# The low parts of the turned tiles: made by GpSimd from a raw copy in SBUF, where VectorE made them from PSUM

## The reference

```python
x = x + tanh(g_xattn[0]) * L0_xattn(ctx, layernorm(x), ...)   # 32 half-heads of 8, att0 - lam * att1
x = x + tanh(g_ffn[0])   * L0_ffn(layernorm(x), ...)          # top 3 of 8 zones, gelu(x @ Wa[e]) @ Wb[e]
x = x + tanh(g_xattn[1]) * L1_xattn(layernorm(x), ctx, ...)   # 16 heads of 16, then @ Wo + bo
x = x + tanh(g_ffn[1])   * L1_ffn(layernorm(x), ...)          # silu(x @ wg.T) * (x @ wu.T) @ wd.T

def layernorm(x):  return (x - mean(x)) / sqrt(var(x) + 1e-5)
```

## Time and profile before

| | |
|---|---|
| median of three runs | 722.27 us |
| profiled execution | 724.65 us |
| its span, first to last instruction | 722.8 us |
| PE busy | 641.1 us (89%) |
| DVE busy | 368.1 us (51%), 814 instructions |
| ACT busy | 370.6 us (51%), 627 instructions |
| POOL busy | 114.3 us (16%), 158 instructions |
| mean granted clock of PE | 0.92 of full |

### The profile page before, as it was taken

How to read it: one execution, slowest core, us unless ns; L and a number is a source line. 1 busy time by engine, 2 the same in 40 slices (tenths; PEclk the granted TensorE clock), 3 DMA queues, 4 the chain that set the end, 5 groups by cost and what they waited for, 6 DMA issues and landing times.

```text
span 722.8 us, 10171 instructions
## 1 busy us (share of the span) xinstructions
PE 641.1 (89%) x3676; PEld 487.8 (67%) x3676; DVE 368.1 (51%) x814; ACT 370.6 (51%) x627; POOL 114.3 (16%) x158
## 2 busy tenths in 40 slices
PE   2377798888889999999999999999888879999996
PEld 2354455545448788888888777787566657888885
DVE  6447566586575352534536535434446655443332
ACT  4124465655666574646657535545753655333332
POOL 8000434334462000000000000000021313000000
PEclk9757899998779999999999999999888878999999
DMA  7301111023003021030203240000161100000000
GB/s 221 87 3 44 46 47 47 18 65 100 3 29 117 2 79 38 0 117 1 89 29 89 64 141 2 1 1 2 26 197 42 47 2 2 0 30 1 29 30 29
DMA packets 22737, 34.66 MB, mean 48 GB/s; under 512 B 4640, under 2 KB 13216, under 8 KB 22688
## 3 DMA queue, kind: packets, MB, share of 16 engines
q1 hardware_dynamic: 21376, 32.87, 15.1%
q10 hardware_dynamic: 864, 0.86, 0.5%
q0 software_dynamic: 448, 0.29, 0.4%
HBM read 18.93 MB, written 2.10 MB: 29 GB/s over the span
## 4 chain that ended last, share of the span: by engine, by line
PE 74%; DVE 8%; ACT 5%; SPq 4%; issue 3%; DMA 3%; POOL 2%; ACTq 1%; DVEq 0%; POOLq 0%
PE SC L1127 27%; PE PV L1127 25%; PE PV L1145 5%; PE SC L1258 4%; PE AUX L1127 4%; PE AUX L1230 3%; DVE NM L1011 3%; SPq L521 2%; SPq L532 2%; DMA QG<-NMT 2%; PE AUX L1186 2%; ACT XN L729 1%; DVE O L1019 1%; ACTq L712 1%; ACT NMT L770 1%
## 5 line engine op out<-in xcount | busy, mean ns | idle before, releaser
L871 DVE TENSOR_TENSOR HL<-HF,HH 128x512 fp32r<-128x512 f32 x120 | 83.3, 695 | 156.2 <-ACT HH L823 156.0
L781 ACT ACTIVATE PB<-SC 77x1024 f32<-77x1024 f32 x96 | 95.1, 1014 | 63.7 <-PE SC L1258 63.3
L823 ACT ACTIVATE HH<-PV 128x512 fp32r<-128x512 f32 x96 | 57.3, 597 | 66.7 <-PE SC L1127 66.7
L1258 PE MATMUL SC<-QG,KA 128*128 128x512 f32 x192 | 75.2, 487 | 16.0 <-DMA QG<-NMT 14.0
L818 ACT ACTIVATE HF<-PV 128x512 f32<-128x512 f32 x96 | 57.5, 599 | 58.4 <-PE PV L1127 56.3
L1127 PE MATMUL PV<-XH,WAH 128*128 128x512 f32 x192 | 78.2, 407 | 1.0 <-DVE O L1019 1.0
L1127 PE MATMUL PV<-XL,WAH 128*128 128x512 f32 x192 | 76.4, 398 | 0.0
L1127 PE MATMUL PV<-XH,WAL 128*128 128x512 f32 x192 | 76.2, 397 | 0.0
L1127 PE MATMUL SC<-HL,WBH 128*128 128x512 f32 x192 | 75.6, 394 | 0.0
L1127 PE MATMUL SC<-HH,WBH 128*128 128x512 f32 x192 | 75.3, 392 | 0.0
L1127 PE MATMUL SC<-HH,WBL 128*128 128x512 f32 x192 | 75.0, 390 | 0.0
(11 more groups left out here) (236 smaller groups left out, 1190.8 us busy)
## 6 DMA issues: line engine op xcount, KB each, us to landing
QG<-QH SPq DMA_DIRECT2D x120, 64.0 KB, 2.0
WSA<-in_wa SPq DMA_DIRECT2D x6, 1024.0 KB, 4.9
WSB<-in_wb SPq DMA_DIRECT2D x12, 512.0 KB, 6.8
QG<-QL SPq DMA_DIRECT2D x60, 64.0 KB, 2.0
X<-in_x SPq DMA_DIRECT2D x4, 512.0 KB, 6.0
out_x<-X SPq DMA_DIRECT2D x4, 512.0 KB, 2.6
WI<-in_wg SPq DMA_DIRECT2D x1, 768.0 KB, 4.4
WI<-in_wu SPq DMA_DIRECT2D x1, 768.0 KB, 6.8
```

Of the source, the lines that this page charges most:

```text
L781: act.activation(probs(n)[0:S, :, :], SC[0:S, n % 2, :, :], ACT.Exp, scale=SCALE[a]).then_inc(exp_done, 1)
L823: act.activation(HH[s % 2][:, :], PV[:, s % 2, :], ACT.Gelu_apprx_tanh).then_inc(act_done, 1)
L871: return dve.tensor_tensor(dst, raw, hi.bitcast(F32), ALU.subtract)
L1258: ins = pe.matmul(SC[:, n % 2, i, :], KALL[a][:, at_h:at_h + P], QG[m % 2][:, h // NS[a], :], start=True, stop=True)
```

## The change

ACT, which copied each half once, now copies it twice: first raw into `XN` (the buffer that the transposes have just read), then rounded into `XH`. The rounded copy frees the bank. Since the raw copies overwrite `XN`, ACT waits until both halves are transposed before it starts. POOL then subtracts, `XL = XN - XH`, from SBUF, and counts a new semaphore `lo_ready`. The users of a turned tile on PE wait for `lo_ready` (`turned`), and so does the next `scale`, which writes `XN` again. DVE has no part in `turn` any more; `turn_mix` keeps its old form.

```diff
+        def turned(eng, stage, j):
+            eng.wait_ge(lo_ready, KC * (order["turn", stage, j] + 1))
 # gpsimd
+                elif kind == "turn":
+                    _, stage, j = step
+                    for c in range(KC):
+                        pool.wait_ge(hi_ready, KC * order[step] + c + 1)
+                        used(pool, step + (c,))
+                        raw = XN[:, KC * c:KC * (c + 1), :].rearrange("p t n -> p (t n)")
+                        lo_part(XL[:, j, c, :], raw, XH[:, j, c, :]).then_inc(lo_ready, 1)
 # scalar
                     for c in range(KC):
                         filled(act, step + (c,))
+                    for c in range(KC):
                         pooled = {"accum_out": POOLED[:, c, j:j + 1]} if stage == FFN0 else {}
-                        act.activation(XH[:, j, c, :], bank(step + (c,)), copy, **pooled).then_inc(hi_ready, 1)
+                        raw = XN[:, KC * c:KC * (c + 1), :].rearrange("p t n -> p (t n)")
+                        act.activation(raw, bank(step + (c,)), copy).then_inc(hi_ready, 1)
+                        act.activation(XH[:, j, c, :], bank(step + (c,)), copy, **pooled).then_inc(frees(step + (c,)), 1)
                 elif kind == "scale":
...
                     if n:
-                        filled(act, ("turn",) + NORMS[n - 1][1:] + (KC - 1,))
+                        act.wait_ge(lo_ready, KC * n)
 # vector
-                elif kind == "turn":
-                    _, stage, j = step
-                    for c in range(KC):
-                        key = step + (c,)
-                        dve.wait_ge(hi_ready, KC * order[step] + c + 1)
-                        lo_part(XL[:, j, c, :], bank(key), XH[:, j, c, :]).then_inc(frees(key), 1)
 # tensor: query, and in the same way route 0, zone and gated
-                    for c in range(KC):
-                        used(pe, ("turn", ATT1 if a else ATT0, j, c))
+                    turned(pe, ATT1 if a else ATT0, j)
```

More of the change, by code:

```diff
@@ L436, in flamingo @@
         var_ready, rstd_ready, xn_ready = sem("var_ready"), sem("rstd_ready"), sem("xn_ready")
-        hi_ready, qh_ready = sem("hi_ready"), sem("qh_ready")
+        hi_ready, qh_ready, lo_ready = sem("hi_ready"), sem("qh_ready"), sem("lo_ready")
         gates_done, lam_sum, lam_exp, coef_done = (sem(n) for n in ("gates_done", "lam_sum", "lam_exp", "coef_done"))
@@ L1268, in _ @@
                     cols = [(c, 2 * b + i) for c in range(KC) for i in range(2)]
-                    for c in range(KC):
-                        used(pe, ("turn", FFN0, 2 * b + 1, c))
+                    turned(pe, FFN0, 2 * b + 1)
                     for i, (c, j) in enumerate(cols):
@@ L1283, in _ @@
                     if z % TOPK == 0 and f == 0:
-                        for c in range(KC):
-                            used(pe, ("turn", FFN0, j, c))
+                        turned(pe, FFN0, j)
                     if nt == 0:
@@ L1334, in _ @@
                         pe.wait_ge(fsplit_done, 2)
-                        for c in range(KC):
-                            used(pe, ("turn", FFN1, j, c))
+                        turned(pe, FFN1, j)
                     if s >= 2:
```

## The result

The four runs of the changed kernel took 740.48, 741.01, 743.48 and 830.90 us, median 742.25, against 722.83 us (median of four) for the kernel before. The ratio is 1.0255, 95% interval 1.0212 to 1.0298: 18.4 us slower (15.3 to 21.5). Ratios leave out executions more than 1.5% above the fastest of their kernel, here the one of 830.90 us at a granted clock of 0.72 (the other three have a median of 741.01) and further on one each in runs 5 and 6 (there the profiled one) and two in run 7, while the medians count them. The forecast was 740.0 in a range of 729 to 747.

What follows compares the result with a forecast made beforehand. PE was taken as nearly full in the zones, with room in ATT0's attention, where low parts' latency counts. Terms sum to 17.75 us, taking the profiled 724.65 to 742.4; against the 722.27 median, 740.0; range 729 to 747.

Steps and rivals of the forecast that it cites:

- First query: ATT0 tile 0: POOL's subtractions stand behind its small DMAs; 2.9 us stall plus 2.4 of slow query, 5.3.
- Tile 1: ATT0 tile 1: four copies free the second bank later for the maxima; 0.5 us, bounds -1.0 to 1.0.
- Tile 2: ATT0 tile 2: query waits 1.7 us for low parts, then runs at the low clock, 2.4 more; 4.1.
- Tile 3: ATT0 tile 3: norm's power late behind POOL's subtractions 1.1, query's wait 1.7, low clock 2.4; 5.2 us.
- Route: FFN0 tile 1: PE's first route waits for `lo_ready`; 1.45 us, bounds 0 and 3.5.
- End of ATT0: FFN0 tile 2's turn: two raw copies on ACT, which is on the chain there; 1.1 us, bounds 0 and 2.
- ATT1's tile 2: ATT1's tile 2 query: low parts come later, clock left out; 1.1 us, bounds 0.8 and 3.5.
- Nine other turns, and HL: Remaining turns: copies in ACT's waits, subtractions covered by PE's products; 0 in sum, bounds -2 and 3; HL delay a rival.
- The third rival: POOL's subtractions hold up DVE's HL in six turns of zones and gated part: 7.7 us more, 747.7; chance 0.07.
- DVE's relief: Subtractions taken off DVE shorten PE's waits for maxima in attention; -1.0 us, bounds 0 and -8.4.
- The rival in which it decides: Start and attention: DVE's saved 13.7 us all shorten the chain, the clock stays up; 720.1 us, chance 0.09.
- a clock that stays up: ATT0's three stalled queries: no low clock follows, so 3 x 2.4 = 7.2 us go; 732.8, chance 0.20.

Runs made afterwards that it cites:

- run 5: Changed kernel, but DVE instead of POOL subtracts the high part from the raw copy in SBUF: 736.5 us, ratio 1.0198.
- run 6: Changed kernel without the raw copies, POOL subtracting from the untransposed tile, so XL holds wrong numbers: 736.2 us, ratio 1.0162.
- run 7: Kernel before plus ACT's raw copies, which nobody reads; DVE still subtracts from PSUM: 733.9 us, ratio 1.0132.
- run 4: Changed kernel, but POOL issues its 13 small DMAs behind the first tile's two subtractions: 741.8 us, ratio 1.0233.
- run 1: Late turns alone: kernel before with only the eight turns of ATT1 and FFN1 changed: 724.4 us, ratio 1.0007.
- run 3: The hybrid: kernel before with only the eight turns that have no user close behind changed: 721.6 us, ratio 0.9978.
- run 10: Kernel before with filling matmuls on PE ahead of waits for moved maxima, three stalls actually filled: 720.6 us, ratio 0.9951.
- run 11: Kernel before with the eight turns that have time changed, plus filling matmuls ahead of waits for moved maxima: 720.0 us, ratio 0.9968.
- run 9: Changed kernel; routes wait for high parts alone, and FFN0 tile 0's update of X stands behind tile 3's power: 735.5 us, ratio 1.0163.
- run 12: Changed kernel, all turns on POOL, with every remedy: subtractions before DMAs, two waits off, stalls filled: 728.1 us, ratio 1.0077.
- run 8: Changed kernel with PE filling matmuls ahead of the queries of ATT0's tiles 0, 2 and 3: 735.4 us, ratio 1.0179.

## Why the prediction was right, and where not

The time came out 1 to 2 us above the forecast and the likeliest case, stalls with a slow PE behind them, is the one that came. Of its terms some were right and some met their size by luck. Measured against the trace of before, cut at the same instructions:

*First query.* Predicted 5.3, as 2.9 of stall and 2.4 of slow matmuls. Measured 5.35: 2.8 more idle, 2.6 more busy. Right in both parts; that most of the stall is owed to POOL's DMAs is shown by run 4.

*Tile 1.* Predicted 0.5; to the second query's QH the lag grew by 0.03, with 0.7 more idle and 0.6 less busy. Right in idle time.

*Tile 2.* Predicted 1.7 + 2.4 = 4.1. Measured 2.8: 1.5 idle, 1.3 busy. The query began fast and was slow only from its third matmul to its tenth, so the clock's price was too high here. The stall looks right, but in part by luck: the old code waits 0.09 us at this query in the trace of before and 1.50 in its other four (runs 1, 3, 10, 11), and it needs 41.2 us for this stretch in the first and 41.6, 43.8 and 41.7 in runs 1, 3 and 10.

*Tile 3.* Predicted 1.1 + 1.7 + 2.4 = 5.2. Measured 6.3: 2.6 idle, 3.7 busy. The sum is near, the step is another: not the query's wait (1.18, not 1.7) put PE to the slow level, but the wait for XN that the late power brought (2.88), one query earlier. Run 9 takes that wait away, and half of the 6.3 goes. The old code alone, in runs 1, 3 and 10, needed 47.5 us for this stretch where the trace of before has 44.78: a slow spell early in it lasts 14 us there and 4 in before. The changed kernel's trace has the short spell too, and run 4's, with the long one, needs 54.16. Like against like the stretch grows by 6.3 and by 6.6 us.

*Route.* Predicted 1.45 of waiting. The step fails as put: PE waited 0.36, and in this stretch idle time fell by 0.3. The lag of 2.5 us is 2.8 of slower matmuls, and they stand ahead of the route. What brings them is open: run 9's trace is without them and run 12's, with the same two edits, is not.

*End of ATT0.* Predicted 1.1 for two copies on ACT. Measured 3.3 in the last stretch (0.4 idle, 2.8 busy), while the one ahead of it gave back 1.4, nearly all busy time. The last stretch does not follow the copies: it takes 22.1 us in run 7 with the copies alone and 23.8 in run 6 without them, against 21.6 before and 24.9 changed (one trace each). Its cause is open. Over the whole kernel the copies were mis-sized: alone they are 9.5 us, about half of the change, where the sizes of the prediction came to 4.6 for them (the expectation of run 5). That they cost their 0.47 or 0.95 us of latency at each turn, and slow PE time behind the stalls that this lengthens, fits runs 5 to 7 and is not shown stall by stall. What I priced at ATT1's tile 2 alone is that both halves must be transposed before the first raw copy, which overwrites XN: on AUX banks ACT waits 8.6 us ahead of raw copies, where it waited 3.6 ahead of high parts.

*ATT1's tile 2.* Predicted 1.1; the wait is 1.13, and the zones' stretch grew by 1.25.

*Nine other turns, and HL.* Predicted 0. Right: the zones kept their busy time (293.31 and 293.43), the gated part its 110.1 us. Inside the zones POOL's subtractions cost nothing that can be seen, and HL's 7 ns more stayed in DVE's waits. The third rival falls. One DVE instruction is held up long, though, WAL beside POOL's XL at the end of ATT0: it took 1.53 us, where WAL took 0.42 in the mean before. The Trainium skill, page "SBUF — State Buffer", section "Who interferes with whom", says that a DVE instruction with two SBUF inputs contends with a GpSimd instruction that reads SBUF; this row agrees in kind:

```profile
216.83 2.50 POOL L589 TENSOR_TENSOR XL<-XN,XH 128x512 fp32r<-128x512 f32 x2
218.09 1.53 DVE L886 TENSOR_TENSOR WAL<-WSA,WAH 128x256 fp32r<-128x256 f32 x1 [4.36 <-ACT WAH L823]
```

*DVE's relief.* Predicted -1.0. Not told from 0: the late turns alone are at +0.5 us (-1.5 to +2.6), the hybrid at -1.6 (-3.7 to +0.6). The rival in which it decides falls.

*The clock.* The prediction put 7.2 us on three queries and gave 0.20 to a clock that stays up. In ATT0 the same PE work took 156.4 to 159.5 us with the old turns and 164.6 to 170.0 with all of ATT0's turns on POOL (three traces each), some 10 us more. With the two waits of run 9 off it is 159.5. So the mechanism stands (run 8). In the three stretches of the late queries it measured 2.6 + 1.3 + 3.7 = 7.6, near the predicted 7.2; 3.6 us more, net, came in the other stretches of ATT0, for which the prediction had nothing. That nearness is partly luck: against run 1's trace, with the same old code, the three stretches hold 3.6 and the others 6.9. The sum of some 10 us is sound, its place is not. The condition, a stall of at least 1.65 us, held ahead of queries: all of 1.94 and more were followed by slow matmuls, none of 1.26 and less where PE had been fast, and those of 1.5 went either way. What it left out is that a PE that is slow already mostly stays slow through a short stall (3 of 4).

All in all: idle time in ATT0 was predicted at 2.9 + 0.5 + 1.7 + 1.1 + 1.7 + 1.45 + 1.1 = 10.45 and measured 7.7, slow work 7.2 against 11.2. The two errors nearly cancel, which is luck and part of why the total is so near. ATT0 ended 18.9 us late, just outside the 15 to 18 that the prediction gave as its sign.

## What to carry to other kernels

A step that lies between PE and PE is priced by its latency, engine queue included, and not by the busy time it moves: 22 us taken off DVE were worth nothing measurable, and two more copies and two slower subtractions per turn in that path cost 18. Price each new stall of PE by its length and by what PE's rate does behind it, and look at the stalls that a late step brings elsewhere as well as at the one that waits for it; ahead of the queries here stalls of up to 1.26 us left a fast PE fast and stalls from 1.94 us on didn't. Filling such a stall with matmuls on a free bank is worth a try: three filled stalls brought the unchanged kernel 3.5 us (0.5%, 0.2 to 0.8%), more than the best placement of these low parts did. Don't read a gain of a few us in one stage off a single pair of traces; the same code differed by 7 us in ATT1.

## What the runs showed of the hardware that was not expected

PE's slow matmuls don't always show in the granted clock of a stretch. The first query of the changed kernel ran at half rate (starts 0.43 us apart for 512 columns, 0.23 elsewhere, as at 1.2 and at 2.4 GHz), and the row of its stretch says 1.00, where the earlier trace rows gave 0.51 for a query of the same length:

```profile
20.20:25.60 5.40, 5.34 (x15) 4.21 (x16) 0.69 (x1) 0.60 (x1) 0.00 (x1) 1.00 0.00 0
```

The spacing of equal matmuls is the surer sign. And single executions differ with the granted clock: 23 runs of the kernel before, in one call, ranged from 718.5 to 726.7 us (in another call to 729.9). The four with a mean granted clock of 0.918 or less took 724.9 to 726.7, the four with 0.927 or more 718.5 to 721.8.
